# Second attention, quantised feed-forward and stores of a two-layer kernel as one unrolled pipeline of 84 steps

## What is computed

```python
x = x + tanh(g_xattn[0]) * L0_attention(layernorm(x), ctx, ctx)      # 16 heads of 8
x = x + tanh(g_ffn[0])   * L0_moe(layernorm(x))                      # 8 experts, the best 2 of each row
x = x + tanh(g_xattn[1]) * L1_attention(layernorm(x), ctx, ctx, mask)  # 16 heads of 64
x = x + tanh(g_ffn[1])   * L1_ffn(layernorm(x))

def L1_ffn(x, w1, conv_w, conv_b, w2):
    h = bit_linear(x, w1)               # 128 -> 512: rows rounded to 8 bits by their largest value, weights to -1, 0, 1
    h = depthwise_conv1d(h, conv_w, conv_b)     # three taps along each sequence of 64
    return bit_linear(silu(h), w2)      # 512 -> 128, rounded again row by row
```

## Time and profile before

| what | us |
|---|---|
| median of three runs | 1902.36 |
| lowest and highest | 1889.66, 1914.15 |
| the profiled execution's own time | 1895.65 |
| its span | 1893.9 |
| mean granted clock of TensorE, share of full speed | 0.946 |
| first attention and router, from 0 to about | 479 |
| experts, until about | 784 |
| second attention, from 789.70 to | 1615.2 |
| statistics and quantised feed-forward, until | 1877.1 |
| the store's landing, until | 1893.9 |

### The profile page before, as it was taken

How to read it: one execution, slowest core, us unless ns; L and a number is a source line. 1 busy time by engine, 2 the same in 40 slices (tenths; PEclk the granted TensorE clock), 3 DMA queues, 4 the chain that set the end, 5 groups by cost and what they waited for, 6 DMA issues and landing times. The chain is left out here.

```text
span 1893.9 us, 39973 instructions
## 1 busy us (share of the span) xinstructions
PE 1660.3 (88%) x13931; PEld 1150.8 (61%) x13931; DVE 1117.5 (59%) x2907; ACT 1067.2 (56%) x1849; POOL 641.1 (34%) x509
## 2 busy tenths in 40 slices
PE   5999999985799999579999999999999999556564
PEld 3777777764477777356666666666666665234443
DVE  5788888664212112156666655666655533899995
ACT  3887777641333333146666666666666555476674
POOL 2336665655000000245444444444444333000000
PEclk9999999775899999779999999999999999799998
DMA  9999900001444444110000000000000000000003
GB/s 307 395 387 376 331 24 24 24 27 39 134 155 142 145 160 143 63 33 26 21 23 21 21 22 22 19 22 21 21 22 23 10 14 7 1 1 1 0 0 90
DMA packets 94943, 156.95 MB, mean 83 GB/s; under 512 B 10416, under 2 KB 41264, under 8 KB 94576
## 3 DMA queue, kind: packets, MB, share of 16 engines
q1 hardware_dynamic: 82512, 128.04, 20.3%
q0 software_dynamic: 11312, 27.02, 4.3%
q10 hardware_dynamic: 1008, 0.40, 0.1%
HBM read 61.84 MB, written 93.59 MB: 82 GB/s over the span
## 5 line engine op out<-in xcount | busy, mean ns | idle before, releaser
L1204 PE MATMUL L1psY<-L1ctxT,L1A 128*128 128x128 f32 x2048 | 253.6, 281 | 7.4 <-ACT L1HT L1452 7.3
L1452 ACT ACTIVATE L1HT<-L1psY 128x512 f32<-128x512 f32 x256 | 152.8, 597 | 181.7 <-PE L1psY L1204 171.7
L1204 PEld LDWEIGHTS L1psY<-L1ctxT,L1A 128*128 128x128 f32 x2048 | 246.3, 196 | 12.7 <-ACT L1HT L1452 9.9
L1219 PE MATMUL L1psY<-L1C,L1ctxV 128*64 128x512 f32 x1024 | 237.7, 598 | 1.9 <-ACT L1V L1459 0.2
L1459 ACT ACTIVATE L1V<-L1psY 128x512 f32<-128x512 f32 x256 | 152.3, 596 | 108.4 <-PE L1psY L1219 107.8
L972 ACT ACTIVATE GhT<-GpsH,Gwx 128x512 f32<-128x512 f32 x156 | 107.2, 687 | 187.1 <-PE GpsH L952 186.5
L1420 POOL TENSOR_TENSOR L1sc<-L1sc,L1rden 128x1024 f32<-128x1024 f32 x64 | 121.8, 1903 | 213.3 <-DVE L1rden L1382 213.1
L1415 POOL TENSOR_TENSOR L1sc<-L1sc,L1top 128x1024 f32<-128x1024 f32 x64 | 123.3, 1926 | 196.4 <-DVE L1top L1373 196.4
L853 POOL TENSOR_TENSOR L0sc<-L0sc,L0top 128x1024 f32<-128x1024 f32 x64 | 121.6, 1900 | 176.5 <-DVE L0top L611 175.0
L988 DVE TENSOR_TENSOR Gyg<-GpsY,Gwx 128x512 f32<-128x512 f32 x39 | 27.0, 692 | 232.6 <-PE GpsY L959 232.6
L1219 PEld LDWEIGHTS L1psY<-L1C,L1ctxV 128*64 128x64 f32 x1024 | 64.2, 136 | 162.8 <-ACT L1V L1459 87.6
(11 more groups left out here) (247 smaller groups left out, 3232.0 us busy)
## 6 DMA issues: line engine op xcount, KB each, us to landing
rows_in<-L0zero SPq DMA_DIRECT2D x1, 34560.0 KB, 96.6
rows_out<-L0zero SPq DMA_DIRECT2D x1, 34560.0 KB
Gwx<-in_experts SPq DMA_DIRECT2D x39, 579.0 KB, 4.2
Gxg<-rows_in SPq DMA_DIRECT2D x39, 256.0 KB, 4.3
rows_out<-Gyg POOLq DMA_DIRECT2D x39, 256.0 KB, 4.4
L1ctxT<-in_ctxT SPq DMA_DIRECT2D x64, 64.0 KB
L1ctxV<-in_ctxT SPq DMA_DIRECT2D x64, 64.0 KB, 1.8
out<-X SPq DMA_DIRECT2D x1, 4096.0 KB, 15.9
```

The lines of the kernel that those rows point to most:

```text
L1204: last = mm(psY[:, c % 2, i * P:(i + 1) * P], A[:, 4 * c + i, :], ctxT[:, u, :], start=True, stop=True)
L1219: last = mm(psY[64 * p:64 * p + 64, c % 2, :], ctxV[:, u, 64 * b:64 * b + 64], C[:, p, 4 * half:4 * half + 4, :], start=True, stop=True)
L1452: nc.scalar.activation(HT[:, u, 4 * c:4 * c + 4, :], psY[:, c % 2, :].rearrange("f (h k) -> f h k", h=4), ACT.Copy).then_inc(s["h_ready"], 1)
```

## The change

- `product` and `take_product` give way to `turn_weight` and `take_weight`: six steps with four transposes each that leave WK, WQ and WV, not multiplied. WO is loaded in four more transfers. The experts' block gets the preparation of VectorE's weights spread over its first turns, and scales WO by the gate.
- Blocks 3 to 6 give way to one block, `attention_ffn`: no loop, 84 steps written out, each with one tile's turn of each stage. Attention runs at lags 0 to 4, the hidden block of the feed-forward at lag 14, its turn at 19, its end at 20; the store of a tile (64 KB) follows at 24.
- The attention is computed by K, Q, V projections with heads of 64: `project_k` and `project_q` (4 matmuls of 128x128 in each of four calls a step), `project_v` (2 matmuls with 64 rows and 512 columns in each of two calls), `scores` and `values` as 32 matmuls of 64x64x64 each, a quarter of the array to each, and `project_out`, eight accumulating matmuls of 128x128.
- Both layer norms of the stage take the reciprocal root from 17 small VectorE operations, without Sqrt. The two clips are gone. GpSimd adds the output's bias (`add_bo`, 128x128) and fetches rows straight from `slot`, without the copy.
- Silu is one ScalarE pass over 128x2048, every fourth step; Exp runs on the same engine every step.
- All of the feed-forward's PSUM tiles share one bank, psF, in the order in which the steps below use it: each waits until the one before has been read.

```diff
+            for k in range(STEPS):
+                ...                    # on TensorE, tile k - lag of each:
+                    project_k(tx, 0)
+                    turn_probs(tt, 0)
+                    turn_probs(tt, 1)
+                    project_k(tx, 1)
+                    turn_x(tx)
+                    hidden(n)
+                    project_q(tx, 0)
+                    values(tt)
+                    project_q(tx, 1)
+                    turn_back(tb)
+                    project_v(tv, 0)
+                    project(tb)
+                    project_v(tv, 1)
+                    scores(tx)
+                    turn_xq((k - FX) // G4)
+                    project_out(tt)
+                    turn_h(th)
+            def scores(t):
+                pe.wait_ge(s["q_ready"], 2 * t + 2)
+                wait(pe, s["scores_out"], t)
+                for j in range(HP):
+                    for p in range(2):
+                        r = slice(64 * p, 64 * p + 64)
+                        for b in range(2):
+                            q = slice(64 * b, 64 * b + 64)
+                            last = mm(psS[q, p, j, :], QT[r, t % 2, j, q], KT[r, t % 2, j, q], start=True, stop=True)
+                last.then_inc(s["scores_ps"], 1)
+            def silu(g):
+                act.wait_ge(s["conv"], FM * g + FM)
+                wait(act, s["t_ps"], G4 * (g - 1))
+                nc.scalar.activation(hs[:, g % 2, :, :], hc[:], ACT.Silu).then_inc(s["hs_ready"], FM)
+            def scales(t):
+                c = slice(t, t + 1)
+                dve.wait_ge(s["am_done"], t + 1)
+                vec.tensor_scalar(step2[:, c], am2[:, c], 1e-5, 1.0 / 127.0, ALU.max, ALU.mult).then_inc(s["step_ready"], 1)
+                dve.wait_ge(s["step_ready"], t + 1)
+                vec.reciprocal(scl2[:, c], step2[:, c]).then_inc(s["scl_ready"], 1)
+                vec.tensor_scalar(inv2[:, c], step2[:, c], wmean[:, 1:2], None, ALU.mult).then_inc(s["inv_ready"], 1)
```

More of the change, by code:

```diff
@@ L93, in normalise_stats @@
[L93 to L129, removed]
@@ L1158, in _ @@
+            for t in range(NT - FB - 4, NT):
+                store(sp, t)
+            sp.wait_ge(s["stored"], 16 * NT)
         @block.tensor
@@ L1241, in turn_probs, with take_bank @@
[L1241 to L1245 removed]
+            freed = {"M": None, "F": None}
+            def take_bank(bank, sem, value):
+                if freed[bank]:
+                    pe.wait_ge(*freed[bank])
+                freed[bank] = (sem, value)
@@ new lines, in hidden, with turn_h @@
+            def hidden(n):
+                g, m = n // FM, n % FM
+                pe.wait_ge(s["xqT_ready"], g + 1)
+                take_bank("F", s["conv"], n + 1)
+                mm(psF[:], W1[:, m * P:(m + 1) * P], xqT[:, g % 2, :], start=True, stop=True).then_inc(s["h_ps"], 1)
+            def turn_h(t):
+                g, i = t // G4, t % G4
+                pe.wait_ge(s["hs_ready"], FM * (g + 1))
+                take_bank("F", s["z_out"], t + 1)
+                for m in range(FM):
+                    last = nc.tensor.transpose(psF[:, m * P:(m + 1) * P], hs[:, g % 2, m, i * P:(i + 1) * P], ident[:])
+                last.then_inc(s["t_ps"], 1)
@@ new lines, in _ @@
+            for k in range(STEPS):
+                tx, tv, to = tile(k, LX), tile(k, LV), tile(k, LO)
+                n, n2, th, tb = tile(k, FH), tile(k, FH + 1), tile(k, FT), tile(k, FB)
+                if to is not None:
+                    add_x(to)
+                if tile(k, LN) is not None:
+                    layernorm(k)
+                for t in collects.get(k, []):
+                    collect(t)
+                small(k, 0)
+                if to is not None:
+                    new_stats(to)
+                small(k, 1)
+                if n is not None:
+                    conv_left(n)
+                    conv_right(n)
+                small(k, 2)
+                if tv is not None:
+                    sums(tv)
+                small(k, 3)
+                if tv is not None:
+                    invert(tv)
+                small(k, 4)
+                if tb is not None:
+                    residual(tb)
+                if tx is not None:
+                    add_bias(tx)
+                    tops(tx)
+                if th is not None:
+                    largest(th)
+                    scales(th)
@@ L1699 @@
+            for t in range(FIRST_FETCHES):
+                fetch(t)
+            for k in range(STEPS):
+                tx, tv = tile(k, LX), tile(k, LV)
+                for t in fetches.get(k, []):
+                    fetch(t)
+                if tv is not None:
+                    normalise(tv)
+                if tile(k, LN) is not None:
+                    add_bo(k)
+                if tx is not None:
+                    shift(tx)
 def kernel(x, ctx_1024, mask_SxS2_ik0, g_xattn, g_ffn, L0_xattn_wq, L0_xattn_bq, L0_xattn_wk, L0_xattn_bk, L0_xattn_wv,
```

1029 lines of the change are left out of this document (448 added, 581 removed).

## The result

| what | before, us | after, us |
|---|---|---|
| median (4 runs each) | 1903.09 | 1932.06 |
| lowest and highest | 1889.66, 1914.15 | 1922.48, 1933.99 |
| ratio, with its 95% interval | | 1.016 (1.0115 to 1.0205) |
| span of the profiled execution | 1893.9 | 1932.3 |
| granted clock over the span | 0.946 | 0.899 |

The changed kernel is slower by 1.6%, 29 us. The forecast was 1950 in a range of 1825 to 1985. So the number held. The interval is clear of no change but reaches past the bound of 2%, so it leaves open whether the kernel counts as the same or as slower by that bound.

A forecast was written before the change was run, and what follows sets the result against it. Bound: TensorE in attention, another engine in feed-forward. Merged, waits at the step's border were to set 17.2 us a step; 784.7 before the stage plus 1166 gave span 1951, forecast 1950 (own range 1920 to 1985; with rivals 1825 to 1985).

The forecast's parts named there:

- 45 full steps: Steps 20 to 64 of the merged pipeline, all stages running: 17.2 us each, 774 in all.
- TensorE per step: TensorE's work in one merged step, summed from instruction prices: 13.8 us, with scores and values at 1.2 a block.
- The chain at the border: At the step's border TensorE idles before Q 0 for rounding and ScalarE's copies: 14.85 us a step without GpSimd's block.
- rival 2: TensorE sets the pace after all, at 13.8 us a step before Silu: 1825 us, faster; chance 0.25.
- The block by GpSimd: The one-column tensor_scalar after largest waits until GpSimd's shift ends: 1.25 us more, a step of 16.1.
- Rival 1: GpSimd doesn't block the one-column tensor_scalar: 56 us less, 1896, no change; chance 0.25.
- if that tensor_scalar is short: Sign against the forecast: the small tensor_scalar after largest takes about 0.15 us, not over 1 us.
- Silu: Every fourth step's table load, Silu pass and load back on ScalarE hold up TensorE: 4.4 us, 1.1 a step.
- The tail: Steps 67 to 83, feed-forward alone: 11 x 7.7 + 6 x 4.5, 112 us; then 3 for the last store.
- The first steps: Steps 1 to 13 of the pipeline, attention alone: 11.9 us each, 155 in all.
- rival 3: The array's quarters don't overlap in scores and values, or written-out code stalls: put at 2030 us; chance 0.12.
- The start: Layer 0 ends 5 us earlier, so the stage starts at 784.7; filling before the first step takes 18.

The follow-up runs named there:

- e4: The changed kernel with the small tensor_scalar after largest made two columns wide instead of one: 1907.66 us, ratio to the kernel before 1.033.
- e2: The changed kernel with Silu written by Tanh, one 128x512 block each step, and a multiplication on VectorE: 1790.29 us, ratio to the kernel before 0.969.
- e8: The changed kernel with five useless matmuls of 512 columns on TensorE in each Silu step, where it would wait: 1901.33 us, ratio to the kernel before 1.007.
- e7: The changed kernel with the hidden block in a bank of psS instead of psF from step 66 on: 1816.74 us, ratio to the kernel before 0.983.
- e3: The changed kernel with filler matmuls into a free bank at three places of each step from 66 on: 1838.7 us, ratio to the kernel before 0.996.
- a0_after: The changed kernel without edit, run again on another chip beside the kernel before: 1866.24 us against 1848.97, ratio 1.0096.
- c3: The changed kernel with both Silu by Tanh block by block and the tail's hidden block in its own bank: 1740.5 us against 1848.97, ratio 0.9397.
- e5: The changed kernel with layernorm of the next tile moved ahead of add_bias: 1938.53 us, ratio to the kernel before 1.026.
- e1: The changed kernel with Silu replaced by a plain ScalarE copy of the same size, without table loads: 1808.31 us, ratio to the kernel before 0.979.

## Why the prediction was right in number and wrong in its working

The forecast's sum against the trace of the changed kernel:

| part | forecast | measured |
|---|---|---|
| start of the run to shift 1 | 814.6 | 828.5 |
| shifts 1 to 13 | 143 | 164.8 |
| shifts 13 to 19 | 84 | 79.6 |
| 45 full steps | 774 | 684.9 |
| tail | 135 | 174.5 |
| span | 1951 | 1932.3 |

- **TensorE per step: 0.5 too high.** 13.8 was the sum, and TensorE is busy 13.26 in a plain step. That the step's 13.73 comes so near to the sum is luck: it is 13.26 and the wait of 0.47. The unseen blocks of 64 took 1.02, or 1.1 from start to start, as the lower bound had it.
- **The chain at the border: right in kind, too long in size.** Rounding ends at 2.10 after K 0 starts (1313.45 to 1315.55), where I had 2.05. But the copies start 0.47 apart (1315.45, 1315.92), not 0.58, so Q 0 starts at 4.27 and not 4.75. From there to the next K 0 (1327.20) it is 9.48, not 10.1. Together 1.1 less than my 14.85: nearly the whole difference to rival 2, whose pace the plain steps have, without its reason. e4 shows that the chain still binds.
- **The block by GpSimd: wrong.** This is the step that failed. I took the nearest kin in the rows, a copy of two columns, for an operation of one, and let it be held up until `shift` ends. The operation took 0.154 us in all 64 steps; e4 shows it blocked with two columns (1.36). That is 1.25 a step, 56 of the 89 us by which the 45 steps were too dear. Rival 1 had this right. By my own signs the prediction was wrong here: "if that tensor_scalar is short".
- **Silu: too cheap.** 6.2 instead of 4.4 in eight of the eleven steps (20.3 less the 14.1 of the same step in e2). ScalarE's share was right (4.3 by e8 and e2); I had left out that TensorE's wait can cost it its clock (1.9).
- **The tail: too cheap by 39.5.** I priced 7.7 a step from the durations at full clock and did not follow the shared bank psF through a step where nothing covers it. e7 puts the bank at 51 us of the tail, e3 the clock at 18; the two overlap.
- **The first steps: too cheap by 22.** I had written-out code's stalls in rival 3, as an alternative to the forecast and not as a term of it. On a chip without them the part is 139.8, near my 143.
- **The start:** 14 late. The first fetch came 4 later than before and not 5 earlier, within what layer 0 varies by; the other 5 are in the filling (33.2 here, 26.6 in a0_after).

So minus 89 and minus 4 met plus 14, 22 and 39.5. The range held by cancellation, which is luck, and the reason for slower that I gave (a blocked operation) is not what made it slower. In the first pair the stage is 34 us longer than before, and the stalled first steps and filling, which a0_after doesn't have, are 32 of them; their cause stays open. Without them the stage is as long as before, and what kept it from being shorter is, by the runs: Silu's pass and its loads in one piece with the clock behind them (e2: 62 us) and the bank that makes the tail a chain (e7: 51 us). What is right in the change is its idea: c3 keeps the pipeline, takes both of these away, and is 6% faster than the kernel before.

## What to carry to other kernels

When stages are merged into one pipeline, price three things that the separate stages never show: a long operation that comes every few steps (spread it over all steps, even at more total work), a resource that is shared only to save room (follow it through the steps where half of the pipeline has run out), and the clock of an engine that is made to wait. Where a price is taken over from a similar instruction, check that its size is on the same side of whatever makes the difference; one column and two were not. And compare stages by an instruction that comes once a step, not by the total: here the stretch ahead of the stage differed by 22 us between two variants with the same code in it.

## What the runs showed of the hardware

- A tensor_scalar from SBUF to SBUF beside a GpSimd operation over 128x1024: 0.154 us with one column, 1.36 with two (e4), 0.85 for 128x128 when it starts 1.1 after the pass. A scalar_tensor_tensor of 128x128 with two inputs from SBUF goes from 0.34 to a mean of 0.98 when it comes to stand there (e5).
- An idle of 2.4 us of TensorE was followed by some 6 us at half the clock in most steps with Silu and by no fall in two of the first (1100.39, 1220.15). Five matmuls of no use in its place kept the clock at 1.00 each time and saved 1.9 us where it had fallen.
- 64 loads and matmuls of 64x64x64 in four quarters of the array take 1.02 us, 16 ns each.
- A table load is followed at once by the operation that needs it (1345.55 + 1.28, Silu at 1346.84), and the two loads of a step cost 2.9 us where they take 2.57 (18.4 in e8 against 15.55 in e1, both at a clock of 1.00).
- One and the same program had TensorE's stream of small instructions broken in its first steps (shifts 1 to 13: 164.8 us against 139.8) on one chip and whole on another, and its variants' broken again on the chip of the third group; the loops of the kernel before took the same time on the two on which they were traced, and the loop over the experts took 280.2 to 281.7 us in the six traces read for it.
